# Hybrid conv, attention and MoE layers on one core: the 5x5 depthwise conv split 16 taps on GpSimd to 9 on TensorE, and ahead of GpSimd's gathers

## The chip, the cores and the metric

One core of a Trainium2 chip. The metric is the device time of one execution in microseconds (us); several executions are timed and the median is given. TensorE does matrix products (PE in the rows, PEld for its weight loads), VectorE is DVE, ScalarE is ACT, GpSimd is POOL, and SyncE (SP) issues most DMAs. Each engine works its own instruction list in order; semaphores join them.

## The reference

Eight images of 128 channels by 32 x 32 pixels (1024 tokens) pass through three layers, all in f32:

```python
# 1. conv block: routed window attention (16 x 16 windows of 4 pixels, each attends to its top 4 windows)
q, kv = x @ wq, x @ wkv
lepe = dwconv5x5(v) + b_lepe            # depthwise, on the value image
x = x + softmax(q k_sel) v_sel + lepe
h1 = relu(dwconv3x3(fc1(x)));  x = x + fc2(h1)
# 2. full attention, 4 heads, scores times a distance mask
t = t + Wo(softmax((q k / sqrt(32)) * mask) v)     # on layernorm(t)
# 3. mixture of experts: 8 experts, top 2 by a softmax router
t = t + sum_e combine[:, e] * (gelu(t @ w1[e]) @ w2[e])   # on layernorm(t)
```

## The kernel before

The images run as a software pipeline. The body of image n (a loop for n = 0 to 5, then bodies 6 and 7 written out) does conv layers 3x3 and fc2, full attention and experts of image n. Beside them it finishes the window attention of image n+1 (called `second`) and starts that of image n+2 (`first`). Ahead of the loop image 0's window attention is done alone, and image 1's is started.

In a body, TensorE goes through `ORDER_B`: `dw` (3x3 conv), `fc1`, `fc2`, the layer norm (`centred`, `var`), `v`, `q`, `k`, 32 units of attention (`scores`, `turned`, and the product with V in `times_values`), `wo`, second layer norm, `router`, then `hidden` and `expert` eight times. Work of the other two images stands between these entries by small tables.

The names that the change touches:

- **The 5x5 conv (lepe).** The value image stands padded in `V_PAD`. TensorE sums taps into psA with diagonal weights (`lepe_taps`), in two passes of channel blocks, eight small matmuls to a tap and pass (a group, L500); one more group per pass adds the raster of x. `LEPE_BEFORE` says how many groups stand ahead of which entry: 6, 6, 6, 5, 3 and 6, or 32 in all for an image. ACT copies the sum out (`lepe_copy`), and SP spreads it into `XLEPE` by 16 DMAs. GpSimd then adds the last 10 taps in `last_taps`, each a TENSOR_SCALAR (L1311) and a TENSOR_TENSOR (L1314) of 128 x 1024. Image 0 has all 25 taps on TensorE.
- **GpSimd's window work** (`window_stage`) for image m: eight gathers (L1283, which wait for the table of windows that SP stores from `KV`), 16 key products (L1296, each pair of buffers summed by DVE L988), value products (L1323, L1331, L1337), and then the taps.
- **DVE** adds window attention and `XLEPE` in `window_residual` (L1054), normalises (L1100, L1185, L1187), and works through the router (L1192 to L1220) up to `comb_ready`, on which TensorE's `combine` (L597) waits. Then it makes the queries, keys and values of the next image from TensorE's projections (L941, L942); the last of these sets off the table's store.
- **The value projection** of image n+2: TensorE's `a_values` (two matmuls, L452) after `hidden` 3, read out by ACT (L717) into `V_PAD`.
- **SP's queue** in a body: spread lepe, load the raster into `XLEPE` (after `x1_ready`), store the table, store the output, load x.

Of the kernel before, what the change touches and what calls it, by code (L numbers as in the profile page):

```python
# [33 lines left out]
PX = 4  # L34
# [63 lines left out]
class ImageRing:  # L98
# [22 lines left out]
ROUTED = ["windows", "logits"] + [("qkv", t, p) for t in range(WTILES) for p in range(PX)] + [("v", 0), ("v", 1)]  # L121
LEPE = [("lepe", b) for b in range(2)]
RING_A = ImageRing([(name, 0) for name in ROUTED],
                   LEPE + [("pv", t) for t in range(TT)] + [("attended", t) for t in range(WTILES)] + ROUTED,
                   lambda name: 2 if name in ROUTED else int(name in LEPE or name[0] == "attended"), 2)

# [78 lines left out]
def hybrid_layers(nc, x, x_by_window, packed, gains, out, table):  # L205
    with ExitStack() as ctx:
# [34 lines left out]
        TAP = KV[:, 0].rearrange("p x c -> p (x c)")  # L241
# [63 lines left out]
        tap_ready, lepe_done = sem("tap_ready"), sem("lepe_done")  # L305
# [34 lines left out]
        def _(sp):  # L340
# [89 lines left out]
        def _(pe):  # L430
# [44 lines left out]
            def lepe_taps(m, groups):  # L475

                for a, tap in groups:
# [6 lines left out]
                    if (a, tap) == (1, 0):  # L484
                        pe.wait_ge(lepe_half_done, 2 * (m + 1))
                        fence(pe)
                    if (a, tap) == (0, TAPS5):
                        pe.wait_ge(raster_in, 16 * (m + 1))
                        fence(pe)
                    dy, dx = divmod(tap, 5)  # L490
                    for c in range(4):
                        for b in range(2):
# [5 lines left out]
                            else:  # L498
                                weights, values = ident[rows, rows], XLEPE[rows, 256 * c:256 * c + 256]
                            mm = pe.matmul(psA[b][32 * c:32 * c + 32, 256 * a:256 * a + 256], weights, values,  # L500
                                           start=tap == 0, stop=tap == TAPS5)
                            if (a, tap) == (0, TAPS5) and c == 3:
                                mm.then_inc(lepe_half_done, 1)
                            if (a, tap) == LEPE_GROUPS[-1] and c == 3:
                                mm.then_inc(a_ready[b], 1)

            def a_first_half(m):
# [5 lines left out]
                for h in range(2):  # L513
                    a_values(m, h)

            def emit(name, n):
# [8 lines left out]
                if kind == "fc2":  # L525
                    pe.wait_ge(h2_ready, 2 * PAIRS * (n + 1))
# [128 lines left out]
            def stages_b_to_d(n, second, first):  # L655

                groups = list(SHARED_GROUPS)
                for name in ORDER_B:
# [17 lines left out]
                    if first is not None:  # L676
# [787 lines left out]
```

## Time and profile before

| | us |
|---|---|
| median of 3 runs | 1850.29 |
| lowest and highest | 1837.47, 1858.68 |
| profiled execution, its own time | 1834.99 |
| its span in the trace | 1833.2 |
| TensorE busy | 1594.0 (87%) |
| GpSimd busy | 1148.6 (63%) |
| VectorE busy | 1091.0 (60%) |
| ScalarE busy | 908.9 (50%) |

The profiled execution's own time holds the span and what lies around it. Busy shares are averages over stages with different limits. A timeline row gives the start, the duration and the instruction, then in brackets how long the engine was idle ahead of it and what released it. Bodies begin at about 168, 393, 601, 809, 1017, 1225, 1432 and 1634 us. Granted clock 1.00 is 2.4 GHz and 0.50 is 1.2 GHz.

### The profile page before, as it was taken

How to read it: one execution, taken by the hardware profiler on the slowest of the kernel's cores; microseconds unless marked ns; L12 is line 12 of the kernel's file. 1: busy time of each engine (PE TensorE's matmuls, PEld its weight loads, DVE VectorE, ACT ScalarE, POOL GpSimd, SP SyncE). 2: the span in 40 equal slices, each digit the busy share in tenths (PEclk: the TensorE clock that was granted, in tenths of full speed). 3: DMA queues.
4: the chain of work that ended last, by engine and by line, in shares of the span. 5: the costliest groups of instructions: out<-in, count | busy, mean ns of one | idle time of the engine just before them, and what ended most of it. 6: DMA issues, size and time to landing. Idle time of an engine off the chain costs nothing.

```text
span 1833.2 us, 47362 instructions
## 1 busy us (share of the span) xinstructions
PE 1594.0 (87%) x19136; PEld 1025.1 (56%) x19136; DVE 1091.0 (60%) x2405; ACT 908.9 (50%) x1241; POOL 1148.6 (63%) x653
## 2 busy tenths in 40 slices
PE   2807889899999989899899989899898989898988
PEld 1503447565666557565566647565565647664665
DVE  3493677555755576555765667565765667432754
ACT  0001269433973269433873259523883349533962
POOL 2593999269972899269971899359981899400000
PEclk9658889999999999999999999999999989899998
DMA  3303000040003000040002100031002100000000
GB/s 124 128 12 119 22 13 2 1 152 14 2 2 126 27 13 2 1 140 25 1 2 98 56 13 2 1 129 33 6 2 71 70 12 2 1 13 1 1 1 12
DMA packets 32316, 66.49 MB, mean 36 GB/s; under 512 B 6241, under 2 KB 19553, under 8 KB 31969
## 3 DMA queue, kind: packets, MB, share of 16 engines
q0 software_dynamic: 9216, 33.56, 5.2%
q1 hardware_dynamic: 22880, 29.80, 5.1%
q8 instruction: 164, 2.69, 0.6%
q14 instruction: 56, 0.45, 0.1%
HBM read 46.56 MB, written 12.58 MB: 32 GB/s over the span
## 4 chain that ended last, share of the span: by engine, by line
PE 68%; DVE 10%; ACT 10%; issue 6%; POOL 5%; SPq 1%; DVEq 0%; DMA 0%; ACTq 0%; POOLq 0%
PE psB L433 17%; PE psB L590 10%; PE psB L561 8%; PE psA L500 6%; PE psA L639 6%; PE psB L608 6%; ACT P L798 3%; PE psB L570 3%; ACT PT L806 3%; DVE STACKED L1159 2%; PE psA L448 2%; POOL KV L1296 2%; DVE TN L1100 2%; PE psB L575 2%; DVE P L1112 1%
## 5 line engine op out<-in xcount | busy, mean ns | idle before, releaser
L1112 DVE CUSTOM_DVE_ANT_0 P<-psB,W 128x1024 f32<-128x1024 f32 x256 | 313.6, 1225 | 143.6 <-PE psB L433 116.7
L1296 POOL TENSOR_TENSOR KV<-KVSEL,Q 128x1024 f32<-128x1024 f32 x120 | 284.4, 2410 | 37.8 <-DVE S L988 22.9
L798 ACT ACTIVATE P<-P,NEGMAX 128x1024 f32<-128x1024 f32 x256 | 293.9, 1148 | 18.3 <-DVE NEGMAX L1120 17.0
L590 PE MATMUL psB<-W,P 128*128 128x128 f32 x2048 | 282.8, 281 | 15.8 <-ACT P L798 13.4
L1331 POOL TENSOR_TENSOR PROD<-PROD 128x1024 f32<-128x1024 f32 x180 | 276.3, 1535 | 14.1
L590 PEld LDWEIGHTS psB<-W,P 128*128 128x128 f32 x2048 | 227.0, 142 | 81.3 <-issue 41.6
L806 ACT ACTIVATE PT<-psB 128x1024 f32<-128x1024 f32 x256 | 261.8, 1023 | 12.1 <-PE psB L590 8.8
L433 PE MATMUL psB<-TN,W 128*128 128x512 f32 (+1 forms) x512 | 250.4, 623 | 12.3 <-DVEq L1162 9.2
L1283 POOL DMA_INDIRECT KVSEL<-window_table,CHOSEN x64 | 60.5, 945 | 309.7 <-DMA window_table<-KV 292.6
L433 PE MATMUL psB<-STACKED 96*128 96x512 f32 x512 | 190.2, 453 | 18.2 <-DVEq L1163 18.2
L1228 DVE SCALAR_TENSOR_TENSOR PT<-psB,PT 128x128 f32<-128x128 f32 x512 | 138.2, 343 | 112.3 <-PE psB L608 112.0
L1314 POOL TENSOR_TENSOR XLEPE<-XLEPE,KV 128x1024 f32<-128x1024 f32 x70 | 167.9, 2399 | 5.8
L561 PE MATMUL psB<-H_PAD,DIAG 32*32 32x512 f32 x4608 | 164.0, 617 | 3.4 <-ACTq L754 2.6
L639 PE MATMUL psA<-PT,V 128*32 128x128 f32 x4096 | 159.9, 278 | 3.3 <-issue 2.2
L853 ACT ACTIVATE P<-psB,W 128x1024 f32<-128x1024 f32 x64 | 71.3, 1114 | 168.6 <-PE psB L433 168.6
L433 PEld LDWEIGHTS psB<-TN,W 128*128 128x128 f32 (+1 forms) x512 | 87.9, 185 | 112.7 <-issue 79.6
L500 PE MATMUL psA<-V_PAD,W 32*32 32x256 f32 x3872 | 134.4, 400 | 14.7 <-issue 10.4
L639 PEld LDWEIGHTS psA<-PT,V 128*32 128x32 f32 x4096 | 97.9, 109 | 82.3 <-issue 82.3
L608 PEld LDWEIGHTS psB<-W,P 128*128 128x128 f32 x1024 | 125.3, 195 | 29.5 <-issue 29.5
L561 PEld LDWEIGHTS psB<-H_PAD,DIAG 32*32 32x32 f32 x4608 | 106.2, 105 | 52.2 <-issue 20.0
L767 ACT ACTIVATE PT<-psB,DW_COLS 128x512 f32<-128x512 f32 x64 | 40.5, 683 | 185.6 <-PE psB L561 183.7
L608 PE MATMUL psB<-W,P 128*128 128x128 f32 x1024 | 126.6, 279 | 3.8 <-ACT PT L859 2.4
(127 smaller groups left out, 2211.7 us busy)
## 6 DMA issues: line engine op xcount, KB each, us to landing
window_table<-KV SPq DMA_DIRECT2D x8, 1024.0 KB, 5.7
X<-x_by_window_dram SPq DMA_DIRECT2D x8, 512.0 KB, 5.0
XLEPE<-x_dram SPq DMA_DIRECT2D x8, 512.0 KB, 4.1
XLEPE<-P SPq DMA_DIRECT2D x128, 32.0 KB, 1.9
out_dram<-PT SPq DMA_DIRECT2D x8, 512.0 KB, 3.5
W<-packed_dram SPq DMA_DIRECT2D x1, 3714.5 KB, 11.5
KVSEL<-window_table,CHOSEN POOLq DMA_INDIRECT x64, 6.2
FC<-packed_dram SPq DMA_DIRECT2D x8, 64.0 KB, 2.1
```

Source lines behind the costliest of these rows:

```text
L433: mm = pe.matmul(ps[:, h * HALF:(h + 1) * HALF], lhs, rhs[:, h * HALF:(h + 1) * HALF], **kw)
L500: mm = pe.matmul(psA[b][32 * c:32 * c + 32, 256 * a:256 * a + 256], weights, values, start=tap == 0, stop=tap == TAPS5)
L561: mm = pe.matmul(banks[q][32 * j:32 * j + 32], DIAG[rows, TAPS3 * (2 * i + parity) + tap, :], H1_PAD[rows, parity, 16 * top + dy:16 * top ...
L590: mm = pe.transpose(ps[:, t * 128:(t + 1) * 128], P[:, i % P_BUFFERS, t * 128:(t + 1) * 128], ident)
L608: mm = pe.matmul(ps[:, t * 128:(t + 1) * 128], HG[:, i % 2, t * 128:(t + 1) * 128], w("w2", 128 * i, 128 * i + 128), **whole)
L639: pe.matmul(psA[s][rows, 0:128], V[:, t, rows], PT[:, (HEADS_C * c + h) % TURNED_BUFFERS, t, :], start=t == 0, stop=t == TT - 1)
L798: act.activation(P[:, b, :], P[:, b, :], ACT.Exp, bias=NEGMAX[:, b, 1:2], accum_out=L[:, q, h:h + 1]).then_inc(p_ready, 1)
L806: act.activation(PT[:, u % TURNED_BUFFERS].rearrange("k t q -> k (t q)"), psB[s][:], ACT.Copy).then_inc(b_free[s], 1)
L1112: dve.tensor_tensor_reduce(P[:, b, :], ps[:], w("band", at, at + TOK), 1.0, -3.0e38, ALU.mult, ALU.max, NEGMAX[:, b, 0:1]).then_inc(free, 1)
L1296: pool.tensor_tensor(PRODUCTS[i % 2].rearrange("p (k c) -> p k c", c=C), KVSEL[:, t, keys, 0:C], Q[:, t, q, :].unsqueeze(1).broadcast_to([ ...
L1314: pool.tensor_tensor(acc, acc, product, ALU.add).then_inc(lepe_done, 1)
L1331: pool.tensor_tensor(into, PROD[:, 0:keys * C], PROD[:, keys * C:2 * keys * C], ALU.add).then_inc(value_step, 1)
```

## The change

`POOL_TAPS` goes from 10 to 16, so TensorE keeps 9 taps and the raster's group: 20 groups for an image in place of 32, and `LEPE_BEFORE` places 6, 5, 0, 4, 2 and 3 of them at the same entries. GpSimd's taps (`first_taps`) come ahead of its gathers of the same image. They sum onto the raster of x, which SP now loads into the second half of `PROD` (`POOL_LEPE`), and TensorE takes their sum in as its raster group, now the first of each pass. The load waits for GpSimd's window attention of the image before (`attended_ready`). The value projection moves from the experts to behind `scores` 4 and 5, and DVE reads it out in place of ACT. `fc2` waits for its inputs two steps at a time.

```diff
-ROUTED = ["windows", "logits"] + [("qkv", t, p) for t in range(WTILES) for p in range(PX)] + [("v", 0), ("v", 1)]
+VALUES = [("v", h) for h in range(2)]
+ROUTED = ["windows", "logits"] + [("qkv", t, p) for t in range(WTILES) for p in range(PX)]
...
-LEPE_GROUPS = [(a, tap) for a in range(LEPE_PASSES) for tap in range(TAPS5 + 1)]
-POOL_TAPS = 10
+POOL_TAPS = 16
+RASTER = TAPS5
+LEPE_GROUPS = [(a, tap) for a in range(LEPE_PASSES) for tap in [RASTER, *range(TAPS5)]]
 SHARED_GROUPS = [(a, tap) for a, tap in LEPE_GROUPS if not TAPS5 - POOL_TAPS <= tap < TAPS5]
-LEPE_BEFORE = {("dw", 0, 0): 6, ("dw", 1, 0): 6, "fc2": 6, ("centred", 0, 0): 5, ("var", 0, 0): 3, "v": 6}
+LEPE_BEFORE = {("dw", 0, 0): 6, ("dw", 1, 0): 5, ("centred", 0, 0): 4, ("var", 0, 0): 2, "v": 3}
+VALUES_BEHIND_SCORES = (4, 5)
...
-        TAP = KV[:, 0].rearrange("p x c -> p (x c)")
+        TAP = KVSEL[:, 1].rearrange("p k c -> p (k c)")[:, 0:TOK]
+        POOL_LEPE = PROD[:, TOK:2 * TOK]
...
             def load_raster(m):
-                if not (isinstance(m, int) and m == 0):
-                    sp.wait_ge(x1_ready, m)
-                sp.dma_start(XLEPE[:], x[bass.ds(m, 1)].rearrange("a c n -> (a c) n")).then_inc(raster_in, 16)
+                image_0 = isinstance(m, int) and m == 0
+                if not image_0:
+                    sp.wait_ge(attended_ready, WTILES * m)
+                sp.dma_start(XLEPE[:] if image_0 else POOL_LEPE, x[bass.ds(m, 1)].rearrange("a c n -> (a c) n")
+                             ).then_inc(raster_in, 16)
...
                 for a, tap in groups:
-                    if (a, tap) == LEPE_GROUPS[0]:
+                    if (a, tap) == (0, RASTER):
...
+                        pe.wait_ge(raster_in, 16 * (m + 1))
+                        if not image_0:
+                            pe.wait_ge(lepe_done, POOL_TAPS * m)
...
-                if kind == "fc2":
-                    pe.wait_ge(h2_ready, 2 * PAIRS * (n + 1))
...
                     for k in range(4 * PAIRS):
+                        if k % 2 == 0:
+                            pe.wait_ge(h2_ready, 2 * PAIRS * n + k // 2 + 1)
...
-                        if name == ("hidden", 3):
-                            for h in range(2):
-                                a_values(first, h)
+                        if name[0] == "scores" and name[1] in VALUES_BEHIND_SCORES:
+                            a_values(first, VALUES_BEHIND_SCORES.index(name[1]))
...
-                    if not (isinstance(m, int) and m == 0):
-                        dve.wait_ge(lepe_done, POOL_TAPS * m)
...
+            def values(m, hy):
...
+                if hy == 0:
+                    dve.wait_ge(lepe_done, POOL_TAPS * (m - 1))
+                s = RING_A.slot(("v", hy))
+                dve.wait_ge(a_ready[s], RING_A.turn(("v", hy), m))
+                for wx in range(2):
+                    dve.tensor_scalar(V_PAD[:, 2 + hy:2 + hy + SIDE:2, 2 + wx:2 + wx + SIDE:2],
+                                      psA[s][:, wx * WINS:(wx + 1) * WINS].rearrange("c (j i) -> c j i", i=WIN_SIDE),
+                                      col("bv_a"), None, ALU.add).then_inc(v_ready, 1)
+                dve.wait_ge(v_ready, PX * m + 2 * hy + 2)
                 dve.sem_inc(a_free[s], 1)
...
-            def last_taps(m):
-
-                pool.wait_ge(lepe_in, 16 * LEPE_DMAS * (m + 1))
+            def first_taps(m):
+
+
+                pool.wait_ge(raster_in, 16 * (m + 1))
                 pool.wait_ge(v_ready, PX * (m + 1))
-                acc = XLEPE[:].rearrange("c (y x) -> c y x", y=SIDE)
+                pool.wait_ge(pv_done, 1)
+                acc = POOL_LEPE.rearrange("c (y x) -> c y x", y=SIDE)
...
+                if t == 0 and not (isinstance(m, int) and m == 0):
+                    pool.wait_ge(pool_lepe_read, m)
...
             def window_stage(m):
 
+                first_taps(m)
                 for t in range(WTILES):
                     gathers(m, t)
...
                     values(m, t)
-                last_taps(m)
```

On GpSimd, before, the loop's turn begins with the gathers (L1283) of image n+2 and its key products (L1296):

```order
L1378 ISA
L1278 REGISTER_ALU
L1283 DMA KVSEL<-window_table,CHOSEN 128x1024 x8
L1290 REGISTER_ALU
L1296 TENSOR_TENSOR KV<-KVSEL,Q 128x1024 x2
```

Now it begins with 16 taps, each a product into `KVSEL` (L1340) and a sum onto `PROD` (L1343):

```order
L1409 ISA
L1331 REGISTER_ALU
L1340 TENSOR_SCALAR KVSEL<-V_PAD,W 128x1024
L1342 ISA
L1343 TENSOR_TENSOR PROD<-PROD,KVSEL 128x1024
```

and the last tap is followed by the gathers (L1310):

```order
L1340 TENSOR_SCALAR KVSEL<-V_PAD,W 128x1024
L1342 REGISTER_ALU
L1343 TENSOR_TENSOR PROD<-PROD,KVSEL 128x1024
L1310 DMA KVSEL<-window_table,CHOSEN 128x1024 x8
L1317 REGISTER_ALU
L1323 TENSOR_TENSOR KV<-KVSEL,Q 128x1024 x2
```

What stood behind the value products of an image now stands ahead of its gathers, and is six taps longer.

On TensorE in the loop, before, the last conv groups (L500) stand between the 3x3 conv and `fc2` (L570, 16 matmuls to a row here):

```order
L500 MATMUL psA0<-V_PAD,W 32x256
L500 MATMUL psA1<-V_PAD,W 32x256
L526 ISA
L546 REGISTER_ALU
L570 MATMUL psB0<-PT,FC2 128x512 x16
```

Now the 3x3 conv (L575) runs up to `fc2` (L586), which waits (L583) for its later inputs half way:

```order
L575 MATMUL psB1<-H1_PAD,DIAG 32x512 x8
L575 MATMUL psB2<-H1_PAD,DIAG 32x512 x8
L560 REGISTER_ALU
L583 REGISTER_ALU
L586 MATMUL psB0<-PT,FC2 128x512 x8
L583 REGISTER_ALU
L586 MATMUL psB0<-PT,FC2 128x512 x8
```

The six groups that stood there are gone, and the one wait ahead of `fc2` has become several.

On DVE in the loop, before, units 4 and 5 of the attention scores (L1112, whose maximum L1120 negates) follow each other:

```order
L1112 ISA P,NEGMAX<-psB2,W 128x1024
L1112 ISA NEGMAX 128x1
L1119 REGISTER_ALU
L1120 TENSOR_SCALAR NEGMAX<-NEGMAX 128x1
L1112 ISA P,NEGMAX<-psB1,W 128x1024
```

Now the read-out of the value projection (L1079) stands between them (L1137 and L1145 are the same score operations):

```order
L1145 TENSOR_SCALAR NEGMAX<-NEGMAX 128x1
L1075 REGISTER_ALU
L1077 ISA
L1079 TENSOR_SCALAR V_PAD<-psA0,W 128x16x16 x2
L1082 ISA
L1137 ISA P,NEGMAX<-psB1,W 128x1024
```

DVE has two of these ahead of unit 5 and two ahead of unit 6.

## Rows read from the trace of the kernel before

**Rows 1.** Page, chain that ended last: shares of the span by engine.

```profile
PE 68%; DVE 10%; ACT 10%; issue 6%; POOL 5%; SPq 1%; DVEq 0%; DMA 0%; ACTq 0%; POOLq 0%
```

**Rows 2.** Chain in order of time, end of body 1 and body 2: start, us, what.

```profile
576.57 1.72 PE psA L452 x4
...
619.52 2.79 PE psA L500 x96
...
631.89 1.68 PE psA L500 x48
...
634.81 7.07 PE psB L570 x32
641.88 2.35 PE psA L500 x80
...
646.14 1.47 PE psA L500 x47
```

**Rows 3.** Image 1's start: GpSimd's timeline, a chain row, the page's raster load.

```profile
141.28 1.06 POOL L1337 TENSOR_TENSOR Q<-Q,SUMS 128x512 f32<-128x512 f32 x1
171.46 0.97 POOL L1283 DMA_INDIRECT KVSEL<-window_table,CHOSEN  x1 [29.13 <-DMA window_table<-KV]
...
221.84 0.75 DVE XR L1140
...
XLEPE<-x_dram SPq DMA_DIRECT2D x8, 512.0 KB, 4.1
```

**Rows 4.** Timeline of GpSimd: the first taps in body 1.

```profile
501.85 1.12 POOL L1311 TENSOR_SCALAR KV<-V_PAD,W 128x1024 f32<-128x1024 f32 x1
503.05 2.40 POOL L1314 TENSOR_TENSOR XLEPE<-XLEPE,KV 128x1024 f32<-128x1024 f32 x1
505.66 1.16 POOL L1311 TENSOR_SCALAR KV<-V_PAD,W 128x1024 f32<-128x1024 f32 x1 [0.21 <-POOL XLEPE L1314]
```

**Rows 5.** Timeline: next gather, last key sum and `fc2`'s residual in body 2.

```profile
581.46 0.99 POOL L1283 DMA_INDIRECT KVSEL<-window_table,CHOSEN  x1 [41.51 <-DMA window_table<-KV]
...
634.97 1.22 DVE L988 TENSOR_REDUCE KVSEL<-KV 128x64 f32<-128x1024 f32 x1 [1.10 <-POOL KV L1296]
...
641.93 0.75 DVE L1140 SCALAR_TENSOR_TENSOR XR<-psB,W,XR 128x512 f32<-128x512 f32 x1 [5.74 <-PE psB L570]
```

**Rows 6.** Windows, attention: us, busy PE PEld DVE ACT POOL, clock; then two rows.

```profile
680.00:744.00 64.00, 62.16 (x794) 44.79 (x792) 44.70 (x107) 61.18 (x90) 59.89 (x37) 1.00 0.01 2
...
682.34 1.10 PE L590 MATMUL psB<-W,P 128*128 128x128 f32 x8 [0.40 <-ACT P L798]
...
L942 DVE TENSOR_TENSOR KV<-psA,W 128x256 f32<-128x256 f32 x64 | 26.5, 415 | 0.0
```

**Rows 7.** Timelines of GpSimd and of DVE, side by side in body 0.

```profile
230.30 3.68 POOL L1323 TENSOR_TENSOR PROD<-KVSEL,S 128x2048 f32<-128x2048 f32 x1 [0.18 <-POOL Q L1331]
230.43 4.10 DVE L1100 TENSOR_TENSOR TN<-TN,SQ 128x512 f32<-128x512 f32 x1 [0.63 <-ACT SQ L791]
```

**Rows 8.** Timeline of DVE: second layer norm and router, body 1; then `combine`.

```profile
549.51 0.69 DVE L1100 TENSOR_TENSOR TN<-TN,SQ 128x512 f32<-128x512 f32 x1 [3.32 <-ACT SQ L791]
...
552.38 0.22 DVE L1192 TENSOR_REDUCE PT<-psB 128x8 f32<-128x64 f32 x1 [1.33 <-PE psB L593]
...
553.83 0.22 DVE L1199 TENSOR_TENSOR PT<-PT 128x64 f32<-128x64 f32 x1
...
556.21 0.17 DVE L1208 TENSOR_TENSOR PT<-PT 128x8 f32<-128x8 f32 x1
...
557.15 0.36 DVE L1215 TENSOR_TENSOR PT<-W,PT 128x64 f32<-128x64 f32 x2
...
557.95 0.23 DVE L1220 TENSOR_TENSOR PT<-PT 128x64 f32<-128x64 f32 x1
...
558.36 1.03 PE L597 MATMUL psB<-W,PT 128*8 128x128 f32 x8
```

**Rows 9.** Windows: stretch after a TensorE pause, columns as in rows 6.

```profile
676.00:678.00 2.00, 2.00 (x10) 1.94 (x9) 1.87 (x4) 1.04 (x1) 1.92 (x2) 0.50 0.00 0
```

More of the change, by code:

```diff
@@ L344, in load_raster @@
             def load_raster(m):
-                if not (isinstance(m, int) and m == 0):
-                    sp.wait_ge(x1_ready, m)
-                sp.dma_start(XLEPE[:], x[bass.ds(m, 1)].rearrange("a c n -> (a c) n")).then_inc(raster_in, 16)
+                image_0 = isinstance(m, int) and m == 0
[3 more added lines that the diff above has]
+                             ).then_inc(raster_in, 16)
             def x_is_free(m):
-                for h in range(2):
-                    sp.wait_ge(a_ready[RING_A.slot(("v", h))], RING_A.turn(("v", h), m - 1))
+                for last in VALUES + ROUTED[-2:]:
+                    sp.wait_ge(a_ready[RING_A.slot(last)], RING_A.turn(last, m - 1))
+                    fence(sp)
                 sp.wait_ge(xsum_ready, m)
@@ L370, in spread_lepe @@
                 sp.wait_ge(lepe_copied, 2 * (m + 1))
+                if not (isinstance(m, int) and m == 0):
+                    fence(sp)
+                    sp.wait_ge(x1_ready, m)
                 for a in range(LEPE_PASSES):
@@ L475, in lepe_taps @@
             def lepe_taps(m, groups):
+                image_0 = isinstance(m, int) and m == 0
+                last_tap = (LEPE_GROUPS if image_0 else SHARED_GROUPS)[-1][1]
+                raster = XLEPE if image_0 else POOL_LEPE
                 for a, tap in groups:
-                    if (a, tap) == LEPE_GROUPS[0]:
+                    if (a, tap) == (0, RASTER):
                         pe.wait_ge(diag_ready, 8)
@@ L498, in lepe_taps @@
                             else:
-                                weights, values = ident[rows, rows], XLEPE[rows, 256 * c:256 * c + 256]
+                                weights, values = ident[rows, rows], raster[rows, 256 * c:256 * c + 256]
                             mm = pe.matmul(psA[b][32 * c:32 * c + 32, 256 * a:256 * a + 256], weights, values,
-                                           start=tap == 0, stop=tap == TAPS5)
-                            if (a, tap) == (0, TAPS5) and c == 3:
+                                           start=tap == RASTER, stop=tap == last_tap)
+                            if (a, tap) == (0, last_tap) and c == 3:
                                 mm.then_inc(lepe_half_done, 1)
-                            if (a, tap) == LEPE_GROUPS[-1] and c == 3:
+                            if (a, tap) == (1, last_tap) and c == 3:
                                 mm.then_inc(a_ready[b], 1)
+                    if (a, tap) == (1, RASTER) and not image_0:
+                        mm.then_inc(pool_lepe_read, 1)
             def a_first_half(m):
@@ L694, in _ @@
             a_first_half(0)
+            for h in range(2):
+                a_values(0, h)
             lepe_taps(0, LEPE_GROUPS)
+            for h in range(2):
+                a_values(1, h)
             for t in range(WTILES):
@@ L709, in a_values @@
             def a_values(m):
-                if not isinstance(m, int):
-                    act.wait_ge(lepe_done, POOL_TAPS * (m - 1))
                 for hy in range(2):
@@ L862, in stages_b_to_d @@
                     gelu(e)
-                    if first is not None and e == 3:
-                        a_values(first)
                     if second is not None and e - 2 in (NEXT_IMAGE, NEXT_IMAGE + 1):
@@ L935, in rows @@
                         dve.wait_ge(table_in, 16 * m)
-                        if not isinstance(m, int):
-                            dve.wait_ge(lepe_done, POOL_TAPS * (m - 1))
                     s = RING_A.slot(("qkv", t, p))
@@ L1171, in stages_b_to_d @@
                         attended(u // HEADS_C - 2)
+                    if first is not None and u in VALUES_BEHIND_SCORES:
+                        values(first, VALUES_BEHIND_SCORES.index(u))
                     if u == PROJECTED + 3:
```

21 lines of the change are left out of this document (9 added, 12 removed).

## Prediction

> **What bounds the kernel now.** I read the chain that ended last first: 68% of the span is TensorE, 5% GpSimd [rows 1]. In a steady body (208 us) the chain runs on TensorE from `dw` to `fc2`, through attention and through the experts. It leaves TensorE in the two layer norms, the q and k stage and the router. In attention TensorE is busy for 62.2 and ACT for 61.2 of 64 us [rows 6], so both are close to the bound. GpSimd stands still for 41.5 us ahead of each image's gathers [rows 5], and that hole is what the change fills. So three places matter: conv groups on TensorE, image 1's start, where GpSimd is late, and the stretch in which GpSimd used to be idle, where DVE works through norm and router.
>
> **Conv groups off TensorE.** A group costs 2.79/6 or 2.35/5 = 0.47 us [rows 2]. All twelve that go would be 5.6 us an image, but they are worth what their place is worth:
> - ahead of `dw` 1: one less. ACT's last evacuation that `dw` 1 needs ends just ahead, so 0.4.
> - ahead of `fc2`: six less. From the end of `dw` (631.89) to `fc2` (634.81) are 2.9 us [rows 2]. The single wait of `fc2` on all of ACT's work would now stand bare; asked for two steps at a time, its first half (3.5 of 7.07 us) needs only evacuations long done, and covers ACT's last four. So 2.9.
> - ahead of `centred` 0 and of `var` 0: one less each. Both places (641.88 and 646.14) are on the chain [rows 2]: 0.5 each.
> - ahead of `v`: three less, worth 0, since `v` waits for DVE's normalisation.
>
> That is 4.3 us in bodies 1 to 6, 26 in all, and 0.5 in body 0, whose first part waits for GpSimd: **26.3 us less**. `fc2` now ends 3.8 us earlier, and DVE's key sums, which stand ahead of its residual on DVE, must be done by then. The last ends at 636.19, and DVE then waits 5.74 us for `fc2` [rows 5]. Of that 3.8 and the 1.7 below go, leaving 0.2; the raster's load no longer stands right ahead of the table's store, which I take as another microsecond. So GpSimd does not become the bound here.
>
> **Value projection.** In the experts its 1.72 us (576.57) are on the chain [rows 2]: in bodies 0 to 5, **10.3 us less**. In attention the same 1.72 us stand behind `scores` 4 and 5, where products with V have not begun and TensorE still waits for ACT, 0.40 us ahead of unit 4 alone [rows 6]. DVE gets four read-outs at about the 0.41 us of L942 [rows 6]; it is busy for 44.7 of 64 us, but units 5 and 6 wait behind them, and ACT's exponentials behind those. Bounds: 0 if the gaps hold it, 3.4 if nothing hides TensorE's and DVE's parts. I take 0.8, nearer to the gaps: **4.8 us more** in six bodies.
>
> **Image 1's start.** Its taps now stand ahead of its gathers. A tap is 1.12 + 0.08 + 2.40 + 0.21 = 3.81 us [rows 4], 16 are 61.0. They need the raster, and its load waits for GpSimd's own last value product of image 0 (142.3), then some 4.1 us [rows 3]. So taps run from 146.5 to 207.5, and gathers that began at 171.5 [rows 3] begin 36 us later. There is no cover: body 0's DVE reaches its residual at 221.84, right behind the last key product [rows 3], and TensorE, whose first conv group also waits for these taps, has less to do until then than GpSimd. **36 us more**, once. Either end is within 3 us.
>
> **Steady state on GpSimd.** From the end of the values (501.85) to the next gathers (581.46) are 79.6 us [rows 4, 5]. The raster's load and 16 taps need 65.5, so gathers still wait for the table.
>
> **The new neighbour of norm and router.** In body 1's times the taps now run from about 506 to 568 instead of 502 to 540. DVE's second norm and router stand at 549 to 558 [rows 8], in every body from 0 to 5 inside the taps. What that does is shown where GpSimd and DVE meet today: L1100, 0.69 us when GpSimd is idle [rows 8], took 4.10 when it was issued 0.13 us behind a 3.68 us product of GpSimd [rows 7]: it ended 0.55 us behind that product's end. It waited for the whole instruction. DVE operations with one operand in PSUM, as `fc2`'s residual at 0.75 us [rows 5], do not show this. Taps hold 3.52 of 3.81 us, so an operation that comes at random waits (1.12^2 + 2.40^2)/(2 x 3.81) = 0.92 us.
> - L1100, second half: on the chain, 0.9.
> - L1187 behind it waits a full tap operation (1.1 or 2.4), with 1.3 us of cover under the router's matmuls: 0.4.
> - L1199, L1208, L1211, L1215 twice, L1218 twice and L1220 have both inputs in SBUF, and TensorE's `combine` follows directly (558.36) [rows 8]. No row shows so small an operation beside GpSimd. Lower bound 0; upper bound 2 x 0.92 + 6 x 1.75 = 12.3, if the first two come at random and each other one finds the next tap operation already begun. Stepping the eight through the taps' alternation from every phase, where a second one slips into the 0.21 us gap now and then, I get 7 to 10, and take 8.4: a lock by instruction has no reason to know sizes.
> - TensorE pauses that much longer ahead of `combine`; after a pause it ran at 1.2 GHz (granted clock 0.50) for two microseconds and more [rows 9]. I take 1.3.
>
> The sum is 11.0 a body, bounds 1.3 and 17, in six bodies **66 us more**.
>
> The Trainium skill (SBUF — State Buffer, "Who interferes with whom") says that a DVE instruction with two SBUF inputs contends with a GpSimd instruction that reads SBUF, and that whichever issues second is blocked until the other has finished. Rows 7 agree for 512 columns; no row here reaches the small operations, for which the page makes no exception. It adds copies and scalar operations with both ends in SBUF: L1209 and L1212 would join, and the same stepping then gives 8.7 for 8.4.
>
> **The sum**, against the profiled execution's own 1835.0: 1835.0 - 26.3 - 10.3 + 4.8 + 36 + 66 = **1905**. The median of the runs is 1850.3/1835.0 = 1.0083 times this execution, so 1921 in its terms, 3.8% slower.
>
> **Rivals.**
> - *Small operations do not wait.* Only L1100 and L1187 do, 1.3 a body: 1835.0 - 26.3 - 10.3 + 4.8 + 36 + 8 = 1847, or 1863 by the median, 0.7% over and no change that can be told. For: all waits in the trace are of 512 columns or more. Against: they last to the end of GpSimd's instruction, which depends on nothing in DVE's. It decides below 2.2 us a body.
> - *Every operation waits for a 2.40 us sum.* Ten of them and 2 of clock, 26 a body: 1839 + 156 = 1995, or 2012. Against: the taps alternate.
> - *The start is absorbed and the groups are worth their full 5.6 us.* 1835 - 39 - 10 + 8 = 1794, or 1809, 2.2% faster. Against: GpSimd's list is in order, and `v` waits for DVE.
> - *GpSimd becomes the bound.* Its cycle is 208 less 14 of spare, 194 us; a body without waits would be about 203. It would need 9 us more, and the forecast's longer bodies only widen the room.
>
> **How the numbers follow.** The forecast has 0.69, small operations that do not wait 0.19, a faster end 0.06, longer waits 0.06. A measurement here can tell about 1%. So slower 0.75, same 0.19, faster 0.06. The range reaches from just under the no-wait rival (1856) to the upper bound of 17 us a body (1839 + 102 = 1941, or 1957).
>
> **What would show it.** Right: L1199 to L1220 last 1.1 to 2.5 us each in the bodies 0 to 5 and their old 0.2 in 6 and 7; from L1192 to `combine` 6 us become about 14; image 1's gathers at 207; `fc2` straight behind `dw`; body 6 shorter than its old self by 4. Wrong: small operations of unchanged length beside running taps; taps that end before L1100; key sums later than `fc2`; or attention longer by several microseconds.

## The result and the profile after

The changed kernel takes 1917.9 us (median of 4 runs, 1912.2 to 1924.4) against 1847.5 us of the kernel before beside it: a ratio of 1.040, 95% interval 1.033 to 1.046. The forecast was 1921. The profiled execution has a span of 1917.9 us, 84.7 more than before's; the forecast in these terms was 70 more. The profiled execution of the kernel before (1835.0 us) lies 12.5 us under its median and that of the changed kernel (1919.7) 1.8 above its own, so some 14 of the 84.7 us are spread between executions.

First the chain that ended last, its shares by engine, from the page. It answers to [rows 1]:

```profile
PE 60%; DVE 11%; POOL 9%; issue 9%; ACT 8%; SPq 1%; DMA 1%; DVEq 0%; ACTq 0%; POOLq 0%
```

TensorE gave up 8 points of the chain, to GpSimd, DVE and pauses. The start of `combine` in each body, read off TensorE's timelines, says in which bodies the time went (the lag is after minus before):

| `combine` of body | 0 | 1 | 2 | 3 | 4 | 5 | 6 | 7 |
|---|---|---|---|---|---|---|---|---|
| before, us | 350.3 | 558.4 | 765.9 | 974.2 | 1182.4 | 1390.7 | 1597.8 | 1792.5 |
| after, us | 398.7 | 616.3 | 834.5 | 1052.8 | 1271.0 | 1489.1 | 1687.9 | 1878.8 |
| growth of the lag, us | 48.4 | 9.5 | 10.7 | 10.0 | 10.0 | 9.8 | -8.3 | -3.8 |

Three things stand out: 48 us in the first body, 10 in each of bodies 1 to 5, and 12 given back in the two bodies in which GpSimd has no taps.

**The start.** GpSimd's timeline of the changed kernel, which answers to [rows 3]:

```profile
142.10 1.06 POOL L1368 TENSOR_TENSOR Q<-Q,SUMS 128x512 f32<-128x512 f32 x1
146.95 1.65 POOL L1340 TENSOR_SCALAR KVSEL<-V_PAD,W 128x1024 f32<-128x1024 f32 x1 [3.79 <-DMA PROD<-x_dram]
...
208.29 0.98 POOL L1310 DMA_INDIRECT KVSEL<-window_table,CHOSEN  x1 [0.82 <-POOL PROD L1343]
```

The last product of image 0, then the raster's load, then 16 taps, then the gathers: 36.8 us later than in [rows 3].

**The router.** DVE's timeline of body 1 from the second layer norm to the router's end, which answers to [rows 8]. The lines 1125, 1219, 1226, 1235, 1242 and 1247 were 1100, 1192, 1199, 1208, 1215 and 1220 before:

```profile
594.31 2.08 DVE L1125 TENSOR_TENSOR TN<-TN,SQ 128x512 f32<-128x512 f32 x1 [0.33 <-DVE XLEPE L1065]
...
597.82 2.55 DVE L1212 TENSOR_TENSOR XR<-XR,TN 128x512 f32<-128x512 f32 x1
...
601.12 1.32 DVE L1214 TENSOR_TENSOR XR<-XR,TN 128x512 f32<-128x512 f32 x1 [0.15 <-DVE TN L1125]
603.32 0.22 DVE L1219 TENSOR_REDUCE PT<-psB 128x8 f32<-128x64 f32 x1 [0.88 <-PE psB L609]
...
604.77 0.23 DVE L1226 TENSOR_TENSOR PT<-PT 128x64 f32<-128x64 f32 x1
607.15 1.31 DVE L1235 TENSOR_TENSOR PT<-PT 128x8 f32<-128x8 f32 x1
...
608.93 0.86 DVE L1238 TENSOR_TENSOR PT<-PT 128x16 f32<-128x16 f32 x1
...
609.91 2.49 DVE L1242 TENSOR_TENSOR PT<-W,PT 128x64 f32<-128x64 f32 x2
612.44 1.20 DVE L1245 TENSOR_TENSOR PT<-PT 128x64 f32<-128x64 f32 x2
613.67 2.40 DVE L1247 TENSOR_TENSOR PT<-PT 128x64 f32<-128x64 f32 x1
```

and GpSimd's timeline of the same microseconds:

```profile
606.08 2.35 POOL L1343 TENSOR_TENSOR PROD<-PROD,KVSEL 128x1024 f32<-128x1024 f32 x1
608.63 1.13 POOL L1340 TENSOR_SCALAR KVSEL<-V_PAD,W 128x1024 f32<-128x1024 f32 x1 [0.21 <-POOL PROD L1343]
609.85 2.34 POOL L1343 TENSOR_TENSOR PROD<-PROD,KVSEL 128x1024 f32<-128x1024 f32 x1
612.39 1.17 POOL L1340 TENSOR_SCALAR KVSEL<-V_PAD,W 128x1024 f32<-128x1024 f32 x1 [0.21 <-POOL PROD L1343]
613.65 2.34 POOL L1343 TENSOR_TENSOR PROD<-PROD,KVSEL 128x1024 f32<-128x1024 f32 x1
```

Put the ends side by side. DVE's 607.15 + 1.31 ends 0.03 us behind GpSimd's 606.08 + 2.35, and 613.67 + 2.40 ends 0.08 behind 613.65 + 2.34. An operation on 64 columns, 0.23 us in [rows 8], lasts as long as GpSimd's instruction has still to go. Of a pair only one waits: L1242 took 2.36 and 0.21 us, L1245 0.23 and 1.06. From L1219 to the end of L1247 are 12.8 us; the same stretch took 5.8 in [rows 8].

**Behind it.** `combine` on TensorE's timeline, then windows of the stretch that follows (columns as in [rows 6]):

```profile
616.26 1.86 PE L613 MATMUL psB<-W,PT 128*8 128x128 f32 x8 [7.21 <-DVEq L1248]
```
```profile
616.00:620.00 4.00, 3.17 (x10) 1.64 (x11) 2.35 (x9) 1.01 (x1) 0.00 (x0) 0.50 0.01 2
620.00:624.00 4.00, 4.00 (x7) 1.81 (x7) 1.24 (x4) 0.00 (x0) 0.00 (x0) 0.59 0.00 0
624.00:628.00 4.00, 4.00 (x23) 2.88 (x22) 1.24 (x4) 1.59 (x2) 0.00 (x0) 1.00 0.00 0
```

TensorE has waited 7.21 us and comes back at a granted clock of 0.50, its lower level, up to about 623: `combine` takes 1.86 us for the 1.03 of [rows 8]. From its start to the end of the next `hidden` are 8.0 us instead of 5.8, 2.2 more.

**fc2.** The chain in order of time, which answers to [rows 2]: `fc2` stands straight behind `dw`.

```profile
682.11 9.74 PE psB L575 x274
691.85 7.07 PE psB L586 x32
```

### The profile page after: what moved, and what is told of

It reads as the page before. It is cut to its first block, busy times and chain, and to the rows that moved or that the text cites. A ratio compares the mean times of both kernels' runs of the same rounds, so it can differ in the third digit from the quotient of the medians.

```text
span 1917.9 us, 44860 instructions
## 1 busy us (share of the span) xinstructions
PE 1591.1 (83%) x17792; PEld 1014.1 (53%) x17792; DVE 1169.9 (61%) x2429; ACT 899.9 (47%) x1217; POOL 1300.9 (68%) x737
## 4 chain that ended last, share of the span: by engine, by line
PE 60%; DVE 11%; POOL 9%; issue 9%; ACT 8%; SPq 1%; DMA 1%; DVEq 0%; ACTq 0%; POOLq 0%
PE psB L443 15%; PE psB L606 10%; PE psB L575 6%; PE psA L655 6%; PE psB L624 5%; PE psA L516 5%; POOL KV L1323 3%; ACT P L815 2%; PE psB L586 2%; ACT PT L823 2%; DVE STACKED L1184 2%; PE psA L458 2%; POOL PROD L1343 2%; DVE TN L1125 2%; DVE P L1137 1%
## 5 line engine op out<-in xcount | busy, mean ns | idle before, releaser
L1137 DVE CUSTOM_DVE_ANT_0 P<-psB,W 128x1024 f32<-128x1024 f32 x256 | 313.5, 1224 | 141.5 <-PE psB L443 112.8
L606 PE MATMUL psB<-W,P 128*128 128x128 f32 x2048 | 284.6, 282 | 10.4 <-ACT P L815 8.8
L1343 POOL TENSOR_TENSOR PROD<-PROD,KVSEL 128x1024 f32<-128x1024 f32 x112 | 266.9, 2383 | 9.3
L443 PE MATMUL psB<-TN,W 128*128 128x512 f32 (+1 forms) x512 | 260.9, 646 | 12.4 <-DVEq L1187 9.3
L1310 POOL DMA_INDIRECT KVSEL<-window_table,CHOSEN x64 | 60.5, 945 | 184.9 <-issue 168.6
L575 PE MATMUL psB<-H_PAD,DIAG 32*32 32x512 f32 x4608 | 168.9, 630 | 3.9 <-ACTq L771 2.6
L1340 POOL TENSOR_SCALAR KVSEL<-V_PAD,W 128x1024 f32<-128x1024 f32 x112 | 132.9, 1187 | 49.6 <-DMA PROD<-x_dram 28.0
L443 PEld LDWEIGHTS psB<-TN,W 128*128 128x128 f32 (+1 forms) x512 | 94.3, 198 | 123.3 <-issue 93.0
L1001 DVE TENSOR_REDUCE S<-KV 128x64 f32<-128x1024 f32 x64 | 77.5, 1219 | 124.7 <-POOL KV L1323 122.2
L624 PEld LDWEIGHTS psB<-W,P 128*128 128x128 f32 x1024 | 123.1, 192 | 29.6 <-issue 29.6
L575 PEld LDWEIGHTS psB<-H_PAD,DIAG 32*32 32x32 f32 x4608 | 107.3, 107 | 56.8 <-issue 26.9
## 6 DMA issues: line engine op xcount, KB each, us to landing
W<-packed_dram SPq DMA_DIRECT2D x1, 3714.5 KB, 11.5
```

The source lines that it names most:

```text
L443: mm = pe.matmul(ps[:, h * HALF:(h + 1) * HALF], lhs, rhs[:, h * HALF:(h + 1) * HALF], **kw)
L575: mm = pe.matmul(banks[q][32 * j:32 * j + 32], DIAG[rows, TAPS3 * (2 * i + parity) + tap, :], H1_PAD[rows, parity, 16 * top + dy:16 * top ...
L606: mm = pe.transpose(ps[:, t * 128:(t + 1) * 128], P[:, i % P_BUFFERS, t * 128:(t + 1) * 128], ident)
L624: mm = pe.matmul(ps[:, t * 128:(t + 1) * 128], HG[:, i % 2, t * 128:(t + 1) * 128], w("w2", 128 * i, 128 * i + 128), **whole)
L1137: dve.tensor_tensor_reduce(P[:, b, :], ps[:], w("band", at, at + TOK), 1.0, -3.0e38, ALU.mult, ALU.max, NEGMAX[:, b, 0:1]).then_inc(free, 1)
L1343: pool.tensor_tensor(acc, acc, product, ALU.add).then_inc(lepe_done, 1)
```

## The experiments

Each run stands against the kernel before on the same chip. A difference from the changed kernel is therefore given twice where it matters: between the medians, and by the two ratios, each to its own kernel before. My theory: the loss is DVE held by GpSimd's taps in the router, and the later start. The rivals: the router slows for another reason, or the loss sits elsewhere, in the value projection or in `fc2`.

**The router with GpSimd quiet.** In the changed kernel GpSimd stops behind 11 of 16 taps until `combine`'s input is ready:

```diff
+TAPS_AHEAD_OF_ROUTER = 11
...
                 for k in range(POOL_TAPS):
+                    if k == TAPS_AHEAD_OF_ROUTER and not isinstance(m, int):
+                        pool.wait_ge(comb_ready, m - 1)
```

> The changed kernel with one wait more on GpSimd: from image 2 on it does 11 taps, then waits until DVE has finished the router of the body (comb_ready), then does the last 5 and the gathers. Theory A (DVE's two-input operations in the second norm and the router wait for GpSimd's taps): L1192's successor to combine goes from 12.9 us back to about 6, the pause's clock loss goes too, some 9 to 10 us in each of six bodies, 1918 to about 1860. The 5 taps that come late end about when the table lands, so they cost at most 2 us a body. Rival B (the router stretch is not where the time went; the late start, the lost cover of conv groups and the read-out in attention are): no gain, or a loss by the later gathers, 1918 to 1945.

Measured: 1857.6 us, ratio 1.004 (1.001 to 1.007), 60 us less than the changed kernel (66 by the ratios). DVE's timeline of its router in body 1, with GpSimd's first tap behind it:

```profile
595.71 0.17 DVE L1236 TENSOR_TENSOR PT<-PT 128x8 f32<-128x8 f32 x1
...
597.44 0.22 DVE L1248 TENSOR_TENSOR PT<-PT 128x64 f32<-128x64 f32 x1
```
```profile
597.92 1.12 POOL L1343 TENSOR_SCALAR KVSEL<-V_PAD,W 128x1024 f32<-128x1024 f32 x1 [12.50 <-DVEq L1249]
```

All operations are back at their old length. GpSimd stood still for 12.5 us for it, and still its gathers began 2.35 us behind its last tap, and 21.6 us behind `combine`, where it was 23.1 in the kernel before: the stop made nobody late there.

**The kernel before with GpSimd busy.** The converse: 10 dummy taps, a multiplication and a sum, go into the 41.5 us in which GpSimd stood still [rows 5], in bodies 0 to 6, one body more than the taps of the changed kernel reach.

```diff
+FILLERS = 10
...
+                for k in range(FILLERS):
...
+                    pool.tensor_scalar(scratch, source, col("lepe_w", 0), 0.0, ALU.mult, ALU.add).then_inc(filled, 1)
+                    pool.wait_ge(filled, done + 1)
+                    pool.tensor_tensor(spare, spare, scratch, ALU.add).then_inc(filled, 1)
+                    pool.wait_ge(filled, done + 2)
```

> The kernel before, nothing changed but that GpSimd does ten more operations pairs of the form of a tap (a scaled copy and a sum, of 128 x 1024, on memory that nobody reads) behind its last tap, in its idle 40 us ahead of the gathers. They feed nothing. Theory A: DVE's L1199 to L1220 stretch to 1 to 2.4 us each, 9 to 10 us a body with the clock's loss, in bodies 0 to 6: 1848 to about 1913. Rival B: nothing waits for them, so no change, 1848 within 1%.

Measured: 1925.1 us, ratio 1.040 (1.033 to 1.047). Nothing else of the change is in it. DVE's timeline shows the same lengths in the same router:

```profile
570.53 0.84 DVE L1213 TENSOR_TENSOR PT<-PT 128x16 f32<-128x16 f32 x1
...
575.26 2.40 DVE L1222 TENSOR_TENSOR PT<-PT 128x64 f32<-128x64 f32 x1
```

A body takes 218.6 us and more, as long as in the changed kernel. GpSimd's taps beside the router are enough for the loss of a steady body.

**Which of GpSimd's instructions hold DVE.** The same place, filled with instructions that read nothing:

```diff
+FILLERS = 32
...
+                for k in range(FILLERS):
...
+                    pool.memset(spare, 0.0).then_inc(filled, 1)
+                    pool.wait_ge(filled, done + 1)
```

> The kernel before, with 32 zero fills of 128x1024 added on GpSimd behind its taps (they write a free half of the product buffer and read nothing; the output stays the reference's), so that GpSimd is busy while DVE works through norm and router. Theory A, what holds DVE is a GpSimd instruction that reads SBUF: the router's operations keep the 0.17 to 0.23 us that they have in the kernel before, and the time stays within 1% of it, 1845 to 1860 us. Theory B, any long instruction on GpSimd holds a DVE operation with two inputs in SBUF: each of the eight small operations waits for a fill, up to 1 us each, 5 to 8 us a body with the clock, 1880 to 1900 us. The Trainium skill (SBUF — State Buffer, "Who interferes with whom") ties the wait to a GpSimd instruction that reads SBUF, which is A.

or with instructions of one input:

```diff
+FILLERS = 28
...
+                for k in range(FILLERS):
...
+                    pool.tensor_scalar(scratch, source, col("lepe_w", 0), 0.0, ALU.mult, ALU.add).then_inc(filled, 1)
+                    pool.wait_ge(filled, done + 1)
```

> The same with 28 scalar operations in place of the fills: each reads one 128x1024 tile in SBUF and writes another, as the multiplying half of a tap does (1.12 us, 0.2 us apart; the output stays the reference's). Theory A, one SBUF input on GpSimd is enough to hold DVE: the eight operations last 0.7 to 1.3 us instead of 0.2, 5 to 6 us a body and about 1 for the clock, in six bodies 36 to 42, so 1885 to 1895 us. Theory B, only the two-input sums of the taps hold DVE and the multiplications between them are harmless: no change, 1845 to 1860 us, and the operations that met a 1.1 us multiplication in the changed kernel were waiting for something else.

The fills: 1852.0 us, ratio 1.004 (1.000 to 1.007), no change that can be told. Here are fills on GpSimd's timeline, and DVE's router beside them in body 1:

```profile
558.50 0.95 POOL L1326 MEMSET PROD<- 128x1024 f32 x1 [0.15 <-POOL PROD L1326]
559.60 0.95 POOL L1326 MEMSET PROD<- 128x1024 f32 x1 [0.15 <-POOL PROD L1326]
560.71 0.95 POOL L1326 MEMSET PROD<- 128x1024 f32 x1 [0.15 <-POOL PROD L1326]
```
```profile
558.80 0.67 DVE L1211 TENSOR_SCALAR PT<-PT 128x8 f32<-128x8 f32 x1
...
559.84 0.74 DVE L1214 CAST PT<-PT 128x16 f32<-128x16 uint32 x1
560.61 0.36 DVE L1217 TENSOR_TENSOR PT<-W,PT 128x64 f32<-128x64 f32 x2
...
561.40 0.22 DVE L1222 TENSOR_TENSOR PT<-PT 128x64 f32<-128x64 f32 x1
```

No operation with two inputs waits for a fill; the eight keep their 0.17 to 0.23 us in every body. But two operations with one input do: L1211, a scalar operation (L1209 before), and L1214, a cast (L1212 before), both 0.17 us in the kernel before. They end with the fill that runs beside them (559.47 and 559.45, 560.58 and 560.55), and so in all of bodies 0 to 6 (0.59 to 0.97 and 0.74 us). From the router to `combine` TensorE takes 9.1 us for 8.0; over seven bodies that is about the 7.8 us by which the medians differ. So the expectation was right on the two-input operations and on the time, and not on these two. Beside taps and scalar operations the same two kept 0.16 to 0.17 us, but there each fell into the gap behind an operation that had just been held.

The scalar operations: 1860.2 us, ratio 1.010 (1.004 to 1.016), between the two theories. One input is enough to hold DVE's two-input operations:

```profile
560.67 1.12 POOL L1326 TENSOR_SCALAR KVSEL<-KVSEL,W 128x1024 f32<-128x1024 f32 x1 [0.20 <-POOL KVSEL L1326]
```
```profile
560.96 0.85 DVE L1213 TENSOR_TENSOR PT<-PT 128x16 f32<-128x16 f32 x1
...
562.33 1.07 DVE L1220 TENSOR_TENSOR PT<-PT 128x64 f32<-128x64 f32 x2
563.44 0.22 DVE L1222 TENSOR_TENSOR PT<-PT 128x64 f32<-128x64 f32 x1
```

L1213 ends with GpSimd's instruction (561.81 and 561.79), but the pair behind it and L1222 pass unheld. From L1102 to the end of the router the body is 3.5 us longer (551.52 to 563.66, where 549.51 to 558.18 was the stretch of [rows 8]), not 6: I had every operation wait, and here each held one opens the way for the next one or two. The Trainium skill (SBUF — State Buffer, "Who interferes with whom") ties the wait of a two-input DVE instruction to a GpSimd instruction that reads SBUF; 0.17 us for L1213 beside fills and 0.85 beside scalar operations agree.

**The start.** The changed kernel without GpSimd's taps of image 1, which are left out of the sum:

```diff
-                first_taps(m)
+                if isinstance(m, int) and m == 1:
+                    pool.wait_ge(pv_done, 1)
+                    pool.sem_inc(tap_ready, POOL_TAPS)
+                    pool.sem_inc(lepe_done, POOL_TAPS)
+                else:
+                    first_taps(m)
```

> The changed kernel without GpSimd's 16 taps of image 1 (that part of image 1's 5x5 conv is left out, all else stands). Theory A holds the start for a pure delay of 36 to 37 us without cover: 1918 to about 1881. Rival (the start is partly hidden, since TensorE and DVE have work of their own there): 15 us or less, 1903 or more.

Measured: 1884.6 us, ratio 1.018 (1.011 to 1.025), 33 us less than the changed kernel (40 by the ratios). The gathers of image 1 are back at 171.68, and from body to body it still takes 218.6 us. The start and the router are separate costs.

**fc2's wait.** The changed kernel with the single wait ahead of `fc2`:

```diff
+                if kind == "fc2":
+                    pe.wait_ge(h2_ready, 2 * PAIRS * (n + 1))
...
-                        if k % 2 == 0:
-                            pe.wait_ge(h2_ready, 2 * PAIRS * n + k // 2 + 1)
```

> The changed kernel with the single wait ahead of fc2 for all of ACT's evacuations, as before. Theory: six conv groups were the cover of that wait; without them fc2 starts some 2.6 us later, since ACT's last four evacuations last 2.65 us, in bodies 1 to 7: about 18 us more, 1936. Rival (fc2 is not on the path, because DVE's key sums end last ahead of its residual): under 5 us.

Measured: 1927.8 us, ratio 1.043 (1.035 to 1.050): 10 us over the changed kernel by the medians, 5 by the ratios, and the intervals overlap. The wait is there, on TensorE's timeline; but look at the end of the router on DVE's, and at GpSimd's last tap of that body:

```profile
689.13 8.80 PE L586 MATMUL psB<-PT,FC 64*128 64x512 f32 x32 [2.51 <-ACTq L771]
```
```profile
610.51 0.36 DVE L1242 TENSOR_TENSOR PT<-W,PT 128x64 f32<-128x64 f32 x2
...
611.29 0.22 DVE L1247 TENSOR_TENSOR PT<-PT 128x64 f32<-128x64 f32 x1
```
```profile
607.36 2.35 POOL L1343 TENSOR_TENSOR PROD<-PROD,KVSEL 128x1024 f32<-128x1024 f32 x1
```

GpSimd's last tap is over at 609.7 and the router's tail comes behind it. A later `fc2` makes the router later too, out of the last taps, and what TensorE lost ahead of `fc2` it got back there: on the mean of bodies 1 to 5 the stretch from the first `dw` to `v` takes 52.0 us for 46.5, and that from the router to `combine` 9.9 for 15.1. In bodies 6 and 7, which have no taps beside the router, nothing comes back: they are 9.3 and 3.5 us longer. In the changed kernel an earlier `fc2` pushed the router into them. A gain ahead of a lock can be eaten by the lock.

**Both costs mended.** GpSimd's stop as above, and of image 1's taps only the 7 that fit into its old hole; TensorE does the other 9 in body 0, which is written out for it:

```diff
+LATE_TAPS = 9
+FIRST_GROUPS = [(a, tap) for a in range(LEPE_PASSES) for tap in [RASTER, *range(TAPS5 - POOL_TAPS + LATE_TAPS)]]
+FIRST_BEFORE = {("dw", 0, 0): 6, ("dw", 1, 0): 6, "fc2": 16, ("centred", 0, 0): 4, ("var", 0, 0): 2, "v": 4}
...
-            with pe.Fori(0, IMAGES - 2) as n:
+            stages_b_to_d(0, 1, 2)
+            with pe.Fori(1, IMAGES - 2) as n:
```

> The changed kernel with two mends: in the loop GpSimd stops behind 11 taps until the router is through, and image 1 gives GpSimd only the 7 taps that fit in the 24 us in which it waited ahead of image 1's gathers, TensorE does the other 9 (18 groups) in body 0. Theory A, the start and the router are separate costs that add up: 1858 (the split alone) less the 33.6 us that leaving image 1's taps out gave, and 18 groups more on TensorE in body 0, of which I take 3 us for the path: 1824 to 1832 us, 1% to 1.5% under the kernel before. Theory B, TensorE is late in body 0 and pays the 18 groups in full, 8.5 us, and the first body's other work comes later: 1833 to 1845 us.

Beside it the same with before's count, 10 taps ahead of the gathers, and before's places for the groups; then no stop is needed:

```diff
-POOL_TAPS = 16
+POOL_TAPS = 10
-LATE_TAPS = 9
+LATE_TAPS = 3
-LEPE_BEFORE = {("dw", 0, 0): 6, ("dw", 1, 0): 5, ("centred", 0, 0): 4, ("var", 0, 0): 2, "v": 3}
+LEPE_BEFORE = {("dw", 0, 0): 6, ("dw", 1, 0): 6, "fc2": 6, ("centred", 0, 0): 5, ("var", 0, 0): 3, "v": 6}
```

> The place without the count: GpSimd keeps the 10 taps that it has in the kernel before, but ahead of its gathers, and TensorE keeps the groups of the kernel before at their places (image 1: 7 taps on GpSimd, as in the run beside it). Ten taps are over before the router begins, so no wait is needed. Theory A, the ten groups an image that six more taps take from TensorE are worth what the prediction took, 4.3 us a body: 26 us over the run beside it, some 1850 us. Theory B, they are worth next to nothing in a steady body (the bodies of the split kernel were no shorter than before's): within 8 us of the run beside it.

Measured: 1827.1 us, ratio 0.991 (0.988 to 0.994), and 1849.4 us, ratio 1.001 (0.998 to 1.005). The mended kernel is faster than both kernels. The groups (twelve; the expectation's ten is a slip) are worth 22 us, 3.4 a steady body: 208.2 us from `combine` to `combine` against 211.6. Ten taps ahead of the gathers, with the values moved too, stand at a ratio of 1.001: the place alone gains nothing that can be told.

**The loop's way back.** In the mended kernel TensorE pauses at the head of each body that it reaches by its loop, and runs at half clock behind that. Its timeline, and a window (columns as in [rows 6]):

```profile
595.14 0.84 PE L521 MATMUL psA<-PROD,W 32*32 32x256 f32 x16 [2.31 <-issue]
...
597.59 4.08 PE L521 MATMUL psA<-V_PAD,W 32*32 32x256 f32 x71 [0.91 <-issue]
```
```profile
598.00:602.00 4.00, 4.00 (x89) 2.40 (x82) 2.53 (x3) 0.00 (x0) 3.74 (x2) 0.50 0.02 4
```

So I wrote TensorE's loop out, in the mended kernel (shown) and in the kernel before, where it is `pe.Fori(0, IMAGES - 2)`:

```diff
-            stages_b_to_d(0, 1, 2)
-            with pe.Fori(1, IMAGES - 2) as n:
+            for n in range(IMAGES - 2):
                 stages_b_to_d(n, n + 1, n + 2)
```

> The mended kernel (stop behind 11 taps, 7 taps for image 1) with TensorE's loop over the bodies written out; the other engines keep their loops. In the mended kernel the stretch from the experts' last product to the first conv of a body is 9.28 us where TensorE's loop goes back (2.31 us of issue, a second pause of 0.91 us, the first groups at half the granted clock) and 2.78 us in body 1, which follows on written-out code. Theory A, the loop's way back is what costs the 6.5 us and shows in the time: 4 ways back less, 26 us, 1797 to 1806 us. Theory B, the pause comes from somewhere else (the written-out code has to be fetched as well), or GpSimd's key sums end the stretch instead: 1820 to 1832 us.

> The kernel before with the same loop of TensorE written out and nothing else changed. There the stretch is 5.86 us at a way back, 3.1 us more than the 2.79 us that its six groups take at full clock. Theory A: 5 ways back less at 3.1 to 3.8 us, 15 to 19 us, so 1827 to 1833 us. Theory B: no change, 1842 to 1852 us. The gap to the mended kernel in the same form says how much of the 17 us between the two belongs to the place of the taps and how much to how each stands at the loop's start.

Measured: the mended kernel 1805.4 us, ratio 0.976 (0.971 to 0.980); the kernel before 1836.1 us, ratio 0.993 (0.991 to 0.996), 11 us where 15 to 19 were expected. Where those 11 us lie its profile can't say: the profiled execution, at 1841.5 us, is the longest of its ten, and its bodies take 208.3 us. In it TensorE's waits for the first layer norm are 26.7 us, where the kernel before has 16.0, so part of what the head of a body gave was spent there. From the view of waits (us in total, times, longest):

```profile
PE psB L582 <- DVEq L1101: 26.7, 8, 4.6
```

In the mended kernel the head of the body on TensorE's timeline has no pause any more; DVE's timeline in front of `fc2`'s residual stands under it:

```profile
601.18 0.66 PE L521 MATMUL psA<-PROD,W 32*32 32x256 f32 x16
601.64 2.39 PE L521 MATMUL psA<-V_PAD,W 32*32 32x256 f32 x80
603.79 8.78 PE L580 MATMUL psB<-H_PAD,DIAG 32*32 32x512 f32 x264
```
```profile
636.82 1.22 DVE L1007 TENSOR_REDUCE KVSEL<-KV 128x64 f32<-128x1024 f32 x1 [1.11 <-POOL KV L1329]
637.96 1.64 DVE L1171 SCALAR_TENSOR_TENSOR XR<-psB,W,XR 128x512 f32<-128x512 f32 x2
```

Its bodies take 202.9 us on the mean of bodies 1 to 5. The residual now follows DVE's last key sum without a gap, 0.6 to 1.3 us behind the end of `fc2` in bodies 1 to 5, and that sum waits for GpSimd, where [rows 5] show 5.74 us of room: in this form GpSimd is the next bound. The gap between the two kernels grew from 17 us to 31.

## Why the prediction was right

The mechanism was right, and the total, though not each of its parts. Term by term, with the runs that measured each:

| term | predicted, us | measured, us |
|---|---|---|
| DVE held in norm and router, with the clock | +66 | +60, by the ratios +66 (GpSimd stopped for the router) |
| image 1's start | +36 | +33, by the ratios +40 (its taps left out); the gathers 36.8 later |
| groups, values, attention together | -31.8 | not measured alone |

What is left for the last row depends on how it is taken: -23 by the medians, -32 by the ratios, -12 by the spans of the profiled executions. That is too wide to test the term; the table of stages below is the better test.

*Conv groups.* 4.3 us a body were taken for the twelve groups; put back into the mended kernel, they cost 3.4. `fc2` stands straight behind `dw`, as forecast. The three groups ahead of `v`, taken as worth nothing, were worth something (below).

*Value projection.* Its 1.72 us are gone from the experts. In attention the time from the first `turned` to the last grew from 72.7 to 73.6 us on the mean of bodies 1 to 5: 1.0, where 0.8 was taken. No run moved it alone.

*The lock.* Predicted were 11.0 us a body: 0.9 + 0.4 for the norm, 8.4 for the small operations, 1.3 for the clock. Read off body 1, the norm cost 0.8 (0.4 on the mean of bodies 1 to 5), the small operations 7.0 (1.14 + 0.69 + 2.13 + 0.84 + 2.17), the clock 2.2: 10.0. L1226 came in a gap between two taps and did not wait, and neither did one of each pair: five of the eight were held. The two terms that were off, by 1.4 down and 0.9 up, partly cancel. The scalar operation and the cast that the prediction let join (L1209 and L1212) fell into gaps here; beside fills they did wait.

*What was not in the sum.* A steady body grew by 10.0 us, not by 5.8 (11.0 + 0.8 - 1.7 - 4.3). TensorE's timelines, cut by stage, say where (us, mean of bodies 1 to 5; a body runs here from the experts' end to the next experts' end; the forecast column puts each term of the prediction into its stage):

| stage | before | after | growth | forecast |
|---|---|---|---|---|
| experts' end to first `dw` | 5.2 | 6.4 | +1.2 | 0 |
| first `dw` to `fc2` | 29.6 | 27.9 | -1.7 | -3.3 |
| `fc2` | 7.1 | 7.1 | 0 | 0 |
| end of `fc2` to `v` | 11.6 | 11.5 | -0.2 | -1.0 |
| `v` to first `turned` | 17.1 | 18.8 | +1.7 | 0 |
| first `turned` to router | 88.5 | 89.9 | +1.4 | +2.1 |
| router to `combine` | 8.0 | 15.1 | +7.1 | +8.4 |
| `combine` to experts' end | 40.9 | 41.6 | +0.7 | -0.4 |

The lock is near its forecast; what was missed stands in other stages, and most of it goes with a lower granted clock. Up to `fc2` half of the 3.3 us is missing. At the head of body 2 TensorE ran at 0.50 from about 661 to 667 us, in the kernel before from 604 to 607; with TensorE's loop written out, which ran that stretch at 1.00, it takes 25.8 us in the mended kernel and 28.9 in the kernel before, 3.0 less. And the three groups ahead of `v` had kept TensorE at work while DVE normalised. Without them `v` follows a pause, and runs at 0.50 (body 2, before, then after with a window of it, columns as in [rows 6]):

```profile
652.66 2.05 PE L582 MATMUL psB<-W,TN 128*128 128x128 f32 x16 [0.36 <-DVEq L1101]
```
```profile
709.87 3.78 PE L598 MATMUL psB<-W,TN 128*128 128x128 f32 x16 [2.71 <-DVEq L1126]
```
```profile
711.00:713.00 2.00, 2.00 (x11) 2.00 (x11) 0.36 (x2) 0.00 (x0) 1.74 (x3) 0.50 0.18 41
```

The pair of mended kernels agrees: 16.5 us from `v` to the first `turned` with these groups, 17.9 without (bodies 2 to 5). The pause itself also grew. TensorE's waits for the first norm over all bodies, in the view of waits (us in total, times, longest), before and then after:

```profile
PE psB L582 <- DVEq L1101: 16.0, 8, 3.8
```
```profile
PE psB L598 <- DVEq L1126: 25.6, 8, 5.6
```

GpSimd's sums of values stand beside that norm in both kernels, and a small shift decides whether L1125 meets them: in body 2 its second half took 2.10 us. Something came back at the end. Bodies 6 and 7 shrank by 12.1 us in place of the 4.7 that my terms give for what stands behind body 5's `combine`; in body 6 the first norm was free (two operations of 0.7 us) where before it was held twice (2.70 and 2.53), and in body 7 `fc2` lost a 2.53 us wait for ACT. So the total was nearer than its parts: 21 us more than forecast in bodies 1 to 5 and 2 more in body 0, less 7 in bodies 6 and 7 and 1.6 behind the last `combine`, make the 14 us between the forecast +70 and the +85 of the spans. That the medians differ by just the forecast 70 is in part luck: the terms were read off a short execution, and misses of both signs cancel.

The rivals: that small operations do not wait fell with the 2.40 us of L1247; a wait of 2.40 for each fell with the gaps; the start was not absorbed. GpSimd did not become the bound in bodies 1 to 5: its gathers of image 3 had 25 us to spare, and DVE still waited 4.4 to 4.9 us for `fc2`. (The 3.8 us by which the prediction has `fc2` end earlier count a group ahead of `centred`, which stands behind `fc2`; without it they are 3.3.) In body 6 DVE's last key sum ended 1.5 us behind `fc2`, and in the mended kernel with its loop written out this happens in every body from 1 to 5.

What stays open: how much of the first norm's extra wait is due to where GpSimd now stands and how much to chance of phase, and why TensorE's pause at the head of a body is longer than before. No run moved only that.

## What to carry to other kernels

Work given to an idle engine is not free if that engine shares something with the one on the critical path: look at what the path's engine does in the hole, not only at how long the hole is. Work taken off TensorE ahead of a wait is not always a gain either: it can leave a pause, and a lower clock behind it. Here the fix was to leave the work in the hole and make it stop for the 12.5 us that matter. A dummy load in the hole of the old kernel shows such a loss before the change is written.

## What the hardware showed

- Beside GpSimd instructions of 1.12 us with one SBUF input, two-input DVE operations of 16 and 64 columns (0.17 and 0.22 us) took up to 0.86 and 0.94 us; beside sums of 2.35 us with two, one of 64 columns took 2.40.
- Beside GpSimd fills of 0.95 us, which only write, two-input DVE operations kept their length, but a scalar operation and a cast with one input in SBUF (0.17 us) took up to 0.97 and 0.74 us.
- The hold goes both ways: between 600 and 605 us of body 1 GpSimd's 1.12 us multiplication took 1.87 and its 2.34 us sum 2.67.
- Where TensorE's loop goes back, its queue paused 1.7 to 2.3 us, and the granted clock behind it was 0.50 for some microseconds (from 604 to 607 us in the kernel before, from 661 to 667 in the changed kernel, from 596 to 605 in the mended one). Written out, the same stretch ran at 1.00 without a pause.
